# Values in the projections' bank, and two more of the short slots' adds on GpSimd

## The chip, the cores and the metric

The kernel runs on one core of a Trainium2 chip. The metric is the device time of one execution in microseconds. The engines are the tensor engine (PE, matmuls), the vector engine (DVE), the scalar engine (ACT), GpSimd (POOL) and SyncE (SP), which here only issues DMAs. Each works through its own queue in order, and they wait for each other on semaphores. PE writes its results into PSUM, in this kernel eight banks of 128 x 512 fp32.

## The reference, cut to what matters

Eight images of 512 channels and 32 x 32 positions. Layer 0 is attention with 8 heads of 64 channels, layer 1 a masked 3 x 3 convolution. The change touches layer 0 alone.

```python
def _L0_conv_ref(x, Wq, bq, Wk, bk, Wv, bv):
    t = x.reshape(B, C, S).transpose(0, 2, 1)
    q = t @ Wq.T + bq
    k = t @ Wk.T + bk
    v = t @ Wv.T + bv
    q = q.reshape(B * NUM_HEADS, S, hd)          # k and v likewise
    scores = jnp.einsum('gqd,gkd->gqk', q, k) / jnp.sqrt(hd)
    attn = jax.nn.softmax(scores, axis=-1)
    wv = jnp.einsum('gqk,gkd->gqd', attn, v)
    ...
x = x + _L0_conv_ref(_gn(x), Wq, bq, Wk, bk, Wv, bv)
x = x + _L1_conv_ref(_gn(x), weight, bias, mask_weight, filter, 1)
```

The plain reshape into B * 8 groups of 1024 rows makes a group out of 128 tokens by 8 segments of 64 channels. Such a group is one slot of the kernel.

## The kernel before, in words

**Slots and units.** Layer 0 is 64 slots, 8 per image (s = 0 to 7), each 128 tokens. A slot has 8 units, one for each segment of the keys. In a unit PE makes two score tiles of 128 x 512 (`scores`, four matmul steps of two each, L735), ACT takes their exponentials into `prob` (L936), and PE weighs the values with them (`weigh`, L761), two units at a time. In slots 0, 1, 4 and 5 PE also projects keys and queries for the next half image (`project_qk`, 12 matmuls in each of units 1, 3, 5 and 7, L684). In slots 2 and 6 it projects the values (`project_value`, the same count, L694). Slots 3 and 7 have no projection: they are the short slots. Fourteen of them count as short in the code below, those of images 0 to 6.

**Maxima.** During slot h PE also makes, for slot h + 1, eight pairs of tiles (`max_pair`, L705) that DVE reduces to row maxima (`max_item`, L1297). The table `MAX_AT` says in which unit, and whether ahead of its scores (place "a") or behind them (place "c"). In a value slot the pairs stand in units 0, 1, 2, 3, 4, 4, 5, 6, in a short slot in units 0, 1, 2, 2, 3, 4, 4, 5. After the last pair DVE makes a minimum (L1301) and a transposition (L1305), ACT gathers the shift row, and a DMA writes it to where the next slot's scores read it.

**Banks.** Banks 0 to 2 hold scores, banks 3 to 5 are a ring, bank 6 takes the weighed values, and bank 7 (`qk_bank`) the key and query projections; in the short slots it is a fourth score bank as well. The ring is shared by maxima, values, denominators (`den_item`, L1318) and statistics. PE's `take` waits on `ring_free` until DVE has given back the item three before. `PER_RING` is the number of items per image, 146, and since that isn't a multiple of three the distance is two for some items at the end of a period. A pair takes two banks at once, before its first matmul. The rotation of the score banks (`score_banks`) begins each short slot with bank 7. In `scores` PE waits for the banks of both tiles of a unit before it issues either.

**Value copy.** DVE copies a projected value tile out of the ring and adds its bias (`value_item`, L1309). It then waits for its own `value_out` before it frees the bank.

**Sums.** The exponentials are summed in two accumulators. The odd tiles' adds (chunks kc = 1 to 7) are POOL's (L1119). The even tiles' adds are DVE's (L1290), except chunks `EVEN_BY_POOL` in short slots, which are POOL's (`add_even`, L1125). DVE's add of chunk kc stands in unit kc + 1 behind that unit's maxima, and that of chunk 7 in unit 0 of the next slot. In a value slot the add of chunk 6 stands in unit 7, ahead of the fourth value copy. ACT waits for the sums before it overwrites a tile of `prob`, and PE before it makes the denominators. The last five slots of the kernel are summed on PE and have no such adds.

**The start.** Ahead of slot 0 PE projects keys, queries and values of the first half image, the values in four groups of 12 matmuls without a pause, then makes the maxima for slot 0, with the first key projections of the second half in between.

Of the kernel before, what the change touches and what calls it, by code (L numbers as in the profile page):

```python
# [25 lines left out]
ALU = mybir.AluOpType  # L26
# [14 lines left out]
HPI = S // TOK  # L41
# [11 lines left out]
EVEN_BY_POOL = (2, 5)  # L53
# [109 lines left out]
def build(nc, x, wqT, wkT, wvT, chan, bv, wcu, const, out):  # L163
# [11 lines left out]
    with top:  # L175
# [3 lines left out]
        def sb(stack, name, shape, dt):  # L179
# [37 lines left out]
            "u_out0", "u_out1", "u_out2", "den_full", "pv_out", "den_out", "den_in", "recip_done", "recip_out", "recip_in", "o_done", "resid_done", "x1_stored", "value_out")}  # L217
# [107 lines left out]
        PER_RING = HPI * (16 + 1) + 2 * HPH + 2  # L325
# [317 lines left out]
        def _(pe):  # L643
# [21 lines left out]
            def project_qk(t, half, which, j, first=False):  # L665
# [5 lines left out]
                if first:  # L671
                    dst = (qk_bank, pv_bank)[j % 2]
                    if which + j > 0:
                        pe.wait_ge(s1["qk_out"], 4 * which + j)
                else:
                    pe.wait_ge(s1["qk_out"], 8 * t + 4 * which + j + 1)
                    if which == 0 and j == 0:
                        pe.wait_ge(s1["exp_done"], 4 + 16 * HPH * (t - 1))
                steps = [(a, b, c) for c in range(NC) for a, b in
# [8 lines left out]
            def project_value(t, half, g):  # L688
                pe.wait_ge(s1["xn_split"], 2 + 4 * (t + 1))
                dst = take()  # L690
# [5 lines left out]
                mm.then_inc(s1["ring_full"], 1)  # L696
# [22 lines left out]
            def scores(h, s, u, part):  # L719

                half, tok = tokens(s)
                for e in range(2):
                    n = 16 * h + 2 * u + e
                    if part == 0:
                        pe.wait_ge(s1["exp_done"], 4 + n + 1 - score_ago[n])
                        if score_turn[n] == 3:
                            pe.wait_ge(s1["qk_out"], 1 + 8 * (h // HPH + 2))
                for n in (2 * part, 2 * part + 1):
# [11 lines left out]
            def sum_prob(h, kc):  # L740

                if kc == 0:
                    pe.wait_ge(s1["qk_out"], 1 + 16 * B)
                    pe.wait_ge(s1["den_out"], h)
# [368 lines left out]
        def _(pool):  # L1113
# [7 lines left out]
            def add_even(h, s, kc):  # L1121
# [3 lines left out]
                nc.gpsimd.tensor_tensor(acc, acc, prob[:, (2 * kc) % 8], ALU.add).then_inc(s1["sum0"], 1)  # L1125
# [128 lines left out]
        def _(dve):  # L1254
# [52 lines left out]
            def value_item(h, half, g):  # L1307
                src = item()
                dve.scalar_tensor_tensor(out=val[half][:, g], in0=src[:], scalar=1.0 / WSCALE, in1=bv_row[:],  # L1309
                                         op0=ALU.mult, op1=ALU.add).then_inc(s1["value_out"], 1)  # L1310
                dve.wait_ge(s1["value_out"], h + 1)
                dve.sem_inc(s1["ring_free"], 1)
# [507 lines left out]
```

## Time and profile before

| | us |
|---|---|
| median of 3 runs | 2551.43 (2547.43 to 2552.20) |
| the profiled execution | 2547.02 |
| its span, first to last instruction | 2545.2 |
| PE busy | 2440.3 (96%) |
| DVE busy | 1947.8 (77%) |
| ACT busy | 1146.8 (45%) |
| POOL busy | 1156.7 (45%) |

Slot 0 of image 0 begins some 73 us into the span, and the convolution follows from about 1792 us on. TensorE's granted clock has a mean of 0.997. A matmul's time in the rows is its latency: back to back ones begin 0.22 apart and last 0.38. Rows of DVE work that follow each other without a wait overlap by some 0.08, so single maxima of 0.68 begin 0.60 apart. "[0.53 <-DVE nmax L1297]" is the idle time of the engine ahead of a row and what ended it.

### The profile page before, as it was taken

The numbers are of one execution on the slowest core, as the hardware profiler recorded it, in microseconds if no ns is written. First come the engines' busy times: TensorE is split into PE (matmuls) and PEld (weight loads), VectorE is DVE, ScalarE is ACT, GpSimd is POOL, SyncE is SP. The second block draws the span as 40 slices with busy tenths as digits, with TensorE's granted clock in tenths as the row PEclk, the third lists the DMA queues.
The fourth block names the chain that finished last, engine by engine and source line by source line (L and its number), as shares of the span: only waits on it lengthen the run. The fifth ranks groups of instructions, "written<-read, shape, count | busy, mean of one in ns | idle before, by whom it ended". The sixth has DMA issues, their size and how long they took to land.

```text
span 2545.2 us, 38904 instructions
## 1 busy us (share of the span) xinstructions
PE 2440.3 (96%) x13768; PEld 916.8 (36%) x13768; DVE 1947.8 (77%) x2617; ACT 1146.8 (45%) x2059; POOL 1156.7 (45%) x998
## 2 busy tenths in 40 slices
PE   6899999999999999999999999988999999999999
PEld 2233333333333333333333333322444444444444
DVE  5887887888888788788878898976856967967415
ACT  4455556555555556555555554565232132132100
POOL 1376577567567657756755764653121030030000
PEclk9999999999999999999999999999999999999999
DMA  4213232131322313213132231322534634633534
GB/s 128 73 53 87 68 99 81 37 106 53 95 76 74 87 47 111 82 45 106 50 98 76 75 110 36 106 71 72 191 135 174 236 132 165 231 133 133 205 110 165
DMA packets 162783, 267.95 MB, mean 105 GB/s; under 512 B 80160, under 2 KB 80288, under 8 KB 162592
## 3 DMA queue, kind: packets, MB, share of 16 engines
q1 hardware_dynamic: 162320, 264.41, 31.5%
q8 instruction: 113, 1.85, 0.3%
q10 hardware_dynamic: 272, 1.05, 0.1%
q14 instruction: 78, 0.64, 0.1%
HBM read 195.54 MB, written 52.69 MB: 98 GB/s over the span
## 4 chain that ended last, share of the span: by engine, by line
PE 76%; DVE 16%; issue 4%; ACT 1%; DMA 1%; POOL 1%; SPq 0%; DVEq 0%; ACTq 0%; POOLq 0%
PE bank L854 29%; PE bank L761 13%; PE bank L684 12%; PE bank L735 12%; DVE nmax L1297 6%; PE bank L694 5%; DVE prob_sum L1290 4%; PE bank L705 4%; DVE val L1309 1%; PE bank L715 1%; DVE xn_lo L1274 1%; DMA q_top<-shift 1%; ACT prob L936 1%; PE bank L748 1%; DVE xn L1367 1%
## 5 line engine op out<-in xcount | busy, mean ns | idle before, releaser
L1297 DVE TENSOR_REDUCE nmax<-bank 128x1 f32<-128x512 f32 x1024 | 650.9, 680 | 201.6 <-PE bank L705 188.5
L936 ACT ACTIVATE prob<-bank 128x512 f32<-128x512 f32 x1024 | 555.2, 594 | 467.1 <-PE bank L735 465.5
L854 PE MATMUL bank<-v,u_slab 128*128 128x512 f16 x3456 | 746.9, 379 | 0.0
L1119 POOL TENSOR_TENSOR prob_sum<-prob_sum,prob 128x512 f32<-128x512 f32 x354 | 489.8, 1384 | 256.7 <-ACT prob L936 254.6
L761 PE MATMUL bank<-prob,val 128*64 128x512 f32 x2048 | 495.9, 605 | 0.0
L854 PEld LDWEIGHTS bank<-v,u_slab 128*128 128x128 f16 x3456 | 338.1, 98 | 406.9 <-issue 0.8
L1290 DVE TENSOR_TENSOR prob_sum<-prob_sum,prob 128x512 f32<-128x512 f32 x326 | 364.2, 1117 | 23.1 <-POOL prob_sum L1125 21.5
L705 PE MATMUL bank<-k_hi,q_hi 64*128 64x512 f16 x1024 | 200.2, 385 | 35.5 <-DVE nmax L1297 34.7
L735 PE MATMUL bank<-q_hi,k_hi 64*128 64x512 f16 x1024 | 196.4, 378 | 26.4 <-ACT prob L936 26.3
L761 PEld LDWEIGHTS bank<-prob,val 128*64 128x64 f32 x2048 | 124.2, 136 | 237.8 <-issue 186.5
L735 PE MATMUL bank<-q_lo,k_hi 64*128 64x512 f16 x1024 | 196.2, 378 | 8.6 <-DMA q_top<-shift 8.5
L684 PE MATMUL bank<-xn_hi,w_hi 128*128 128x512 f16 x512 | 196.2, 383 | 7.8 <-DVE xn_lo L1274 7.8
L735 PE MATMUL bank<-q_top,spare 64*128 64x512 f16 x1024 | 196.0, 377 | 0.0
L735 PE MATMUL bank<-q_hi,k_lo 64*128 64x512 f16 x1024 | 195.8, 377 | 0.0
L684 PE MATMUL bank<-xn_lo,w_hi 128*128 128x512 f16 x512 | 195.0, 381 | 0.0
L684 PE MATMUL bank<-xn_hi,w_lo 128*128 128x512 f16 x512 | 194.8, 381 | 0.0
L924 ACT ACTIVATE qk<-bank,prm 128x512 f32<-128x512 f32 x128 | 87.9, 687 | 207.7 <-PE bank L684 207.7
L266 POOL TENSOR_TENSOR rstd<-ve,fixed 128x4 f32<-128x4 f32 (+1 forms) x12 | 17.4, 1450 | 337.5 <-DVE ve L247 337.5
L705 PEld LDWEIGHTS bank<-k_hi,q_hi 64*128 64x128 f16 x1024 | 53.1, 93 | 321.5 <-DVE nmax L1297 161.8
L1131 POOL TENSOR_TENSOR den_sb<-pv_sb,den_sb 128x512 f32<-128x512 f32 x64 | 95.2, 1488 | 155.7 <-DMA den_sb<-recip_scratch 155.1
L1119 POOL TENSOR_TENSOR prob_sum<-prob 128x512 f32<-128x512 f32 x59 | 74.7, 1265 | 180.9 <-ACT prob L936 177.9
L1002 ACT ACTIVATE y<-bank 128x512 f32<-128x512 f32 x48 | 28.3, 597 | 276.0 <-PE bank L854 250.4
(146 smaller groups left out, 2876.5 us busy)
## 6 DMA issues: line engine op xcount, KB each, us to landing
u_slab<-u_scratch SPq DMA_DIRECT2D x72, 1024.0 KB, 4.7
xs<-x SPq DMA_DIRECT2D x28, 1024.0 KB, 5.5
tile<-x_scratch SPq DMA_DIRECT2D x26, 1024.0 KB, 6.5
u_scratch<-u_w SPq DMA_DIRECT2D x96, 192.0 KB, 2.9
den_sb<-recip_scratch SPq DMA_DIRECT2D x128, 128.0 KB, 2.9
x_scratch<-xr SPq DMA_DIRECT2D x16, 1024.0 KB, 4.3
xr<-x SPq DMA_DIRECT2D x15, 1024.0 KB, 7.8
res<-x_scratch SPq DMA_DIRECT2D x14, 1024.0 KB, 7.3
```

What stands on the lines that cost most here:

```text
L684: mm = pe.matmul(dst[:], a[:, w, c, j * P:(j + 1) * P], b[:, half, c], start=(n == 0), stop=(n == len(steps) - 1))
L694: mm = pe.matmul(dst[:], a[:, half, c, g * TOK:(g + 1) * TOK], b[:, 2, c], start=(n == 0), stop=(n == len(steps) - 1))
L705: pe.matmul(dst[e][:].rearrange("p (k t) -> p k t", t=TOK), q_hi[half][rows, n // 2, tok], k_hi[half][rows, NC * part:NC * part + NC, tok] ...
L735: mm = pe.matmul(dst[:].rearrange("p (j t) -> p j t", t=TOK), k_op, q_op, start=(n == 0), stop=(n == 3))
L761: pe.matmul(pv_bank[e * D:(e + 1) * D, :], val[s // HPH][:, s % HPH, kc * D:(kc + 1) * D], prob[:, (2 * kc + e) % 8], start=(kc == 0), sto ...
L854: mm = pe.matmul(bank_at(pos, co)[:].rearrange("p (i n) -> p i n", i=2), slab[:, l, c, co * P:(co + 1) * P], image[v][:, 2 * c:2 * c + 2, ...
L924: act.activation(qk32[:, j % 2], src[:], ACT.Identity, bias=prm[:, col:col + 1], scale=1.0 / WSCALE).then_inc(s1["qk_full"], 1)
L936: act.activation(prob[:, (2 * u + e) % 8], score_bank[score_turn[16 * h + 2 * u + e]][:], ACT.Exp, scale=float(D) ** -0.5).then_inc(s1["ex ...
L1119: nc.gpsimd.tensor_tensor(acc, in0, prob[:, (2 * kc + 1) % 8], ALU.add).then_inc(s1["sum1"], 1)
L1131: nc.gpsimd.tensor_tensor(den_sb[:], pv_sb[:], den_sb[:], ALU.mult).then_inc(s1["o_done"], 1)
L1290: dve.tensor_tensor(acc, in0, prob[:, (2 * kc) % 8], ALU.add).then_inc(s1["sum0"], 1)
L1297: dve.tensor_reduce(nmax[:, seg, part:part + 1], src[:], AX.X, ALU.max, negate=True)\
```

## The change

Three edits. First, the value projections write into bank 7 in place of a ring bank. PE waits there for the last query projection to be copied out (`qk_out`) and for the value tile before (`value_out`); DVE waits on a semaphore of its own (`value_ready`) and no longer frees a ring bank. Second, whoever uses bank 7 next waits for the last value copy: the next half's first projection, the short slot's scores in bank 7, and the sums on PE of the last slots. The ring has 138 items per image. Third, POOL takes the even adds of chunks 1, 2, 4 and 5 in short slots; the add of chunk 1 reads `prob` twice, as the first of a sum.

```diff
-EVEN_BY_POOL = (2, 5)
+EVEN_BY_POOL = (1, 2, 4, 5)
...
-        PER_RING = HPI * (16 + 1) + 2 * HPH + 2
+        PER_RING = HPI * (16 + 1) + 2
...
                     if which == 0 and j == 0:
                         pe.wait_ge(s1["exp_done"], 4 + 16 * HPH * (t - 1))
+                        pe.wait_ge(s1["value_out"], 4 * t)
...
             def project_value(t, half, g):
                 pe.wait_ge(s1["xn_split"], 2 + 4 * (t + 1))
-                dst = take()
+                pe.wait_ge(s1["qk_out"], 1 + 8 * (t + 1))
+                pe.wait_ge(s1["value_out"], 4 * t + g)
+                dst = qk_bank
...
-                mm.then_inc(s1["ring_full"], 1)
+                mm.then_inc(s1["value_ready"], 1)
...
                         if score_turn[n] == 3:
                             pe.wait_ge(s1["qk_out"], 1 + 8 * (h // HPH + 2))
+                            pe.wait_ge(s1["value_out"], 4 * (h // HPH + 2))
...
                     pe.wait_ge(s1["qk_out"], 1 + 16 * B)
+                    pe.wait_ge(s1["value_out"], B * HPI)
...
-                nc.gpsimd.tensor_tensor(acc, acc, prob[:, (2 * kc) % 8], ALU.add).then_inc(s1["sum0"], 1)
+                in0 = prob[:, 0] if kc == 1 else acc
+                nc.gpsimd.tensor_tensor(acc, in0, prob[:, (2 * kc) % 8], ALU.add).then_inc(s1["sum0"], 1)
...
             def value_item(h, half, g):
-                src = item()
-                dve.scalar_tensor_tensor(out=val[half][:, g], in0=src[:], scalar=1.0 / WSCALE, in1=bv_row[:],
+                dve.wait_ge(s1["value_ready"], h + 1)
+                dve.scalar_tensor_tensor(out=val[half][:, g], in0=qk_bank[:], scalar=1.0 / WSCALE, in1=bv_row[:],
                                          op0=ALU.mult, op1=ALU.add).then_inc(s1["value_out"], 1)
-                dve.wait_ge(s1["value_out"], h + 1)
-                dve.sem_inc(s1["ring_free"], 1)
```

PE at the turn from a value slot to a short slot, before: the end of the fourth value projection, unit 0's max pair, and the first scores.

```order
500 L694 MATMUL bank<-w_lo,xn_hi 128x512
501 L694 MATMUL bank<-w_hi,xn_lo 128x512
502 L705 MATMUL bank<-k_hi,q_hi 128x512 [waits ring_free,qk_split,qk_moved]
503 L705 MATMUL bank<-k_hi,q_hi 128x512
504 L735 MATMUL bank<-q_hi,k_hi 128x512 [waits exp_done,qk_out]
505 L735 MATMUL bank<-q_hi,k_hi 128x512
506 L735 MATMUL bank<-q_hi,k_lo 128x512 x2
```

And of the change, the same place:

```order
500 L697 MATMUL bank<-w_lo,xn_hi 128x512
501 L697 MATMUL bank<-w_hi,xn_lo 128x512
502 L708 MATMUL bank<-k_hi,q_hi 128x512 [waits ring_free,qk_split,qk_moved]
503 L708 MATMUL bank<-k_hi,q_hi 128x512
504 L739 MATMUL bank<-q_hi,k_hi 128x512 [waits value_out,exp_done,qk_out]
505 L739 MATMUL bank<-q_hi,k_hi 128x512
506 L739 MATMUL bank<-q_hi,k_lo 128x512 x2
```

The order is the same. The first score matmul of the short slot has a third semaphore to wait for, `value_out`.

PE ahead of slot 0, where the second of the four value projections begins, before and then of the change:

```order
109 L694 MATMUL bank<-w_lo,xn_hi 128x512
110 L694 MATMUL bank<-w_hi,xn_lo 128x512
111 L694 MATMUL bank<-w_hi,xn_hi 128x512 [waits ring_free,xn_split]
112 L694 MATMUL bank<-w_lo,xn_hi 128x512
113 L694 MATMUL bank<-w_hi,xn_lo 128x512
```

```order
109 L697 MATMUL bank<-w_lo,xn_hi 128x512
110 L697 MATMUL bank<-w_hi,xn_lo 128x512
111 L697 MATMUL bank<-w_hi,xn_hi 128x512 [waits value_out,qk_out,xn_split]
112 L697 MATMUL bank<-w_lo,xn_hi 128x512
113 L697 MATMUL bank<-w_hi,xn_lo 128x512
```

In place of the ring's `ring_free` it waits for the copy of the tile before, `value_out`.

POOL in a short slot, before, up to the odd add of chunk 7, which stands in the next slot (L1119 odd tiles, L1125 even tiles, L1131 the division for the slot before, L1138 its residual):

```order
63 L1119 TENSOR_TENSOR prob_sum<-prob 128x512 [waits sum1,exp_done]
64 L1125 TENSOR_TENSOR prob_sum<-prob_sum,prob 128x512 [waits sum0,exp_done]
65 L1119 TENSOR_TENSOR prob_sum<-prob_sum,prob 128x512 [waits sum1,exp_done] x3
66 L1125 TENSOR_TENSOR prob_sum<-prob_sum,prob 128x512 [waits sum0,exp_done]
67 L1119 TENSOR_TENSOR prob_sum<-prob_sum,prob 128x512 [waits sum1,exp_done]
68 L1131 TENSOR_TENSOR den_sb<-pv_sb,den_sb 128x512 [waits recip_in,pv_out]
69 L1119 TENSOR_TENSOR prob_sum<-prob_sum,prob 128x512 [waits sum1,exp_done]
70 L1138 TENSOR_TENSOR xr<-xr,den_sb 128x4x128 [waits o_done]
71 L1119 TENSOR_TENSOR prob_sum<-prob_sum,prob 128x512 [waits sum1,exp_done]
```

And of the change (L1124 odd, L1131 even, L1137 and L1144 the division and the residual):

```order
63 L1131 TENSOR_TENSOR prob_sum<-prob 128x512 [waits sum0,exp_done]
64 L1124 TENSOR_TENSOR prob_sum<-prob 128x512 [waits sum1,exp_done]
65 L1131 TENSOR_TENSOR prob_sum<-prob_sum,prob 128x512 [waits sum0,exp_done]
66 L1124 TENSOR_TENSOR prob_sum<-prob_sum,prob 128x512 [waits sum1,exp_done] x2
67 L1131 TENSOR_TENSOR prob_sum<-prob_sum,prob 128x512 [waits sum0,exp_done]
68 L1124 TENSOR_TENSOR prob_sum<-prob_sum,prob 128x512 [waits sum1,exp_done]
69 L1131 TENSOR_TENSOR prob_sum<-prob_sum,prob 128x512 [waits sum0,exp_done]
70 L1124 TENSOR_TENSOR prob_sum<-prob_sum,prob 128x512 [waits sum1,exp_done]
71 L1137 TENSOR_TENSOR den_sb<-pv_sb,den_sb 128x512 [waits recip_in,pv_out]
72 L1124 TENSOR_TENSOR prob_sum<-prob_sum,prob 128x512 [waits sum1,exp_done]
73 L1144 TENSOR_TENSOR xr<-xr,den_sb 128x4x128 [waits o_done]
74 L1124 TENSOR_TENSOR prob_sum<-prob_sum,prob 128x512 [waits sum1,exp_done]
```

Two even adds join, those of chunks 1 and 4, each ahead of the odd add of its chunk.

## Rows read from the trace of the kernel before

**Rows 1.** The page's first part: busy time, share of the span and instructions.

```profile
PE 2440.3 (96%) x13768; PEld 916.8 (36%) x13768; DVE 1947.8 (77%) x2617; ACT 1146.8 (45%) x2059; POOL 1156.7 (45%) x998
```

**Rows 2.** Stretches, image 3's slots 2, 3, 5, 6, 7: length, engines' busy time, clock.

```profile
769.86:799.31 29.45, 28.72 (x172) 9.68 (x169) 25.76 (x35) 19.46 (x37) 23.88 (x24) 1.00 0.16 42
799.31:818.81 19.50, 18.03 (x124) 5.86 (x121) 16.89 (x27) 9.67 (x21) 11.50 (x10) 1.00 0.31 94
...
847.35:875.84 28.49, 28.48 (x172) 9.74 (x169) 21.06 (x31) 17.34 (x36) 20.27 (x19) 1.00 0.52 152
875.84:905.34 29.50, 28.59 (x171) 9.77 (x168) 24.89 (x34) 16.83 (x31) 15.29 (x12) 1.00 0.11 27
905.34:925.16 19.82, 18.02 (x123) 5.94 (x119) 17.22 (x28) 9.66 (x21) 9.13 (x8) 1.00 0.19 68
```

**Rows 3.** Timeline of PE, image 4, slots 2 and 3: start, length, instruction, idle before.

```profile
994.85 0.38 PE L694 MATMUL bank<-w_hi,xn_hi 128*128 128x512 f16 x1 [0.17 <-DVEq L1320]
...
999.31 0.39 PE L705 MATMUL bank<-k_hi,q_hi 64*128 64x512 f16 x2 [0.53 <-DVE nmax L1297]
...
1011.79 0.38 PE L694 MATMUL bank<-w_hi,xn_lo 128*128 128x512 f16 x1
...
1012.33 0.38 PE L735 MATMUL bank<-q_hi,k_hi 64*128 64x512 f16 x2
...
1017.19 0.39 PE L705 MATMUL bank<-k_hi,q_hi 64*128 64x512 f16 x2 [0.78 <-DVE nmax L1297]
```

**Rows 4.** Timeline of DVE, image 4, slots 2 and 3.

```profile
997.63 0.69 DVE L1309 SCALAR_TENSOR_TENSOR val<-bank,bv_row 128x512 f32<-128x512 f32 x1 [0.79 <-PE bank L694]
998.47 1.29 DVE L1297 TENSOR_REDUCE nmax<-bank 128x1 f32<-128x512 f32 x2
...
1009.70 3.43 DVE L1290 TENSOR_TENSOR prob_sum<-prob_sum,prob 128x512 f32<-128x512 f32 x2
1013.06 0.68 DVE L1309 SCALAR_TENSOR_TENSOR val<-bank,bv_row 128x512 f32<-128x512 f32 x1
...
1021.80 3.79 DVE L1297 TENSOR_REDUCE nmax<-bank 128x1 f32<-128x512 f32 x6 [0.74 <-PE bank L705]
```

**Rows 5.** Timeline of DVE, image 1, end of slot 2: the fourth value copy.

```profile
371.88 0.69 DVE L1309 SCALAR_TENSOR_TENSOR val<-bank,bv_row 128x512 f32<-128x512 f32 x1
```

**Rows 6.** Timeline of PE, image 1, slot 3 and slot 7: the pair of unit 2.

```profile
376.88 0.39 PE L705 MATMUL bank<-k_hi,q_hi 64*128 64x512 f16 x2 [0.79 <-DVE nmax L1297]
...
483.78 0.39 PE L705 MATMUL bank<-k_hi,q_hi 64*128 64x512 f16 x2 [1.14 <-DVE nmax L1297]
```

**Rows 7.** Timeline of DVE, slot 7 of image 1 and of image 4: fourth value copy.

```profile
479.65 0.68 DVE L1309 SCALAR_TENSOR_TENSOR val<-bank,bv_row 128x512 f32<-128x512 f32 x1
...
1118.87 0.68 DVE L1309 SCALAR_TENSOR_TENSOR val<-bank,bv_row 128x512 f32<-128x512 f32 x1
```

**Rows 8.** Timeline of PE, image 4, slots 6 and 7.

```profile
1108.71 0.38 PE L694 MATMUL bank<-w_hi,xn_hi 128*128 128x512 f16 x1 [0.22 <-DVE nmax L1297]
...
1123.00 0.39 PE L705 MATMUL bank<-k_hi,q_hi 64*128 64x512 f16 x2 [0.58 <-DVE nmax L1297]
```

**Rows 9.** Timeline of PE ahead of slot 0: first and last value matmul, next projection.

```profile
45.28 0.38 PE L694 MATMUL bank<-w_hi,xn_hi 128*128 128x512 f16 x1
...
55.42 0.38 PE L694 MATMUL bank<-w_hi,xn_lo 128*128 128x512 f16 x1
...
56.05 0.39 PE L684 MATMUL bank<-xn_hi,w_hi 128*128 128x512 f16 x1
```

**Rows 10.** Timeline of DVE ahead of slot 0: last query's split, fourth value copy.

```profile
46.84 0.69 DVE L1282 TENSOR_TENSOR q_lo<-qk,q_hi 128x512 f16<-128x512 f32 x1 [1.90 <-ACT q_hi L927]
...
55.84 0.69 DVE L1309 SCALAR_TENSOR_TENSOR val<-bank,bv_row 128x512 f32<-128x512 f32 x1 [0.99 <-PE bank L694]
```

**Rows 11.** Timeline of POOL, image 4, slot 3: the even add of chunk 5.

```profile
1029.57 1.26 POOL L1125 TENSOR_TENSOR prob_sum<-prob_sum,prob 128x512 f32<-128x512 f32 x1 [3.06 <-DVE prob_sum L1290]
```

**Rows 12.** Line L1290's instructions: DVE's adds, duration in ns, min/median/max.

```profile
L1290 DVE TENSOR_TENSOR prob_sum<-prob_sum,prob x326: 659/1020/1792, 86.9 to 1666.7; 128x512 f32<-128x512 f32 x163
```

More of the change, by code:

```diff
@@ L216, in build @@
             "u_in", "u_act", "u_pool",
-            "u_out0", "u_out1", "u_out2", "den_full", "pv_out", "den_out", "den_in", "recip_done", "recip_out", "recip_in", "o_done", "resid_done", "x1_stored", "value_out")}
+            "u_out0", "u_out1", "u_out2", "den_full", "pv_out", "den_out", "den_in", "recip_done", "recip_out", "recip_in", "o_done", "resid_done", "x1_stored", "value_ready", "value_out")}
         def statistics(dve, signal, step, cols):
```

## The prediction, made before the changed kernel had run

> **What bounds the kernel now.** I read the page first: the tensor engine (PE) is busy for 2440.3 of 2545.2 us [rows 1]. A gain can only come out of the idle time that is left on it. The table of stretches by slot puts that time in its place [rows 2]. In image 3, slot 5 lasts 28.49 us with PE busy for 28.48, so nothing can be won there. Slots 2 and 6, the ones with value projections, last 29.45 and 29.50 with 0.73 and 0.91 idle. The short slots 3 and 7 last 19.50 and 19.82 with 1.47 and 1.80 idle. Some 5 us of idle time per image, 40 in all, is what the change can reach at most; part of it is the turn from a short to a long slot, which the change leaves as it is.
>
> The timeline of PE names the waits [rows 3, 6, 8]. In image 4's slot 2 a value projection waits 0.17 for a ring bank that the copy of the denominators holds, and the max pair of unit 4 waits 0.53 for the vector engine (DVE). In slot 3 the first max pair of unit 2 waits 0.78 (0.79 in image 1), in slot 7 of image 4 0.58 and in slot 7 of image 1 1.14, all for a DVE max. In slot 6 one more value projection waits 0.22, where the ring's period ends and its banks come round after two items. So PE is held by DVE's lateness around the turn from the value slot to the short slot. The timeline of DVE shows why it is late: the value copy of unit 7 comes behind two adds of 1.7 us each [rows 4, 7], where the same add takes 0.66 at best [rows 12].
>
> **Part 1, values in the projections' bank, in the value slots.** PE issues the same matmuls in the same order. Gone is the ring's wait before each value projection, and gone is DVE's wait for its own copy before it gives a ring bank back: from the copy at 997.63 to the next max at 998.47 are 0.84 [rows 4], where back to back ones are 0.60 apart, so 0.24 per copy.
> - First wait of slot 2: the start comes 0.17 sooner by the idle time shown, 0.24 by the distance of starts. I take 0.24.
> - The max pair of unit 4 still needs the bank of unit 4's first pair, the ring being three deep, and DVE reads that one after the value copy. It was released 0.84 after DVE began on it (998.47 to 999.31, rows 3 and 4). With the projection 0.24 earlier and 0.24 of sync gone it begins at 997.99, so the pair starts at 998.83, or 0.48 sooner than now. This stall is halved, not removed.
> - Slot 6 has the same two and the 0.22 (0.29 by starts): 0.77.
>
> So PE reaches the end of slot 2 about 0.48, and of slot 6 about 0.77, sooner.
>
> **Part 1, at the start of the short slots.** Here the change adds a wait. The four-bank rotation of a short slot begins with bank 7, and both score tiles of unit 0 wait before either is issued. They now wait for the value copy out of bank 7. Queued behind that wait on PE are all scores, the sums of the slot before and the next max pairs; the scalar engine (ACT) waits for those scores. The price: PE's last value matmul starts at 1011.79 and the first score at 1012.33 [rows 3]. A value copy starts at 55.84 after its last matmul's start at 55.42 [rows 9, 10], 0.42 later, and DVE gives a bank back 0.84 after it began (above), so the score starts 1.26 after the matmul at the best, against 0.54: at least 0.72 lost in each of 14 short slots. Where DVE is late it is more.
>
> What it covers is the later wait for the max. Call V the start of unit 7's value copy. Now the pair of unit 2 starts at V + 4.13 (1013.06 and 1017.19; 1118.87 and 1123.00; 479.65 and 483.78) [rows 3, 4, 7, 8], in image 1's slot 3 at V + 5.00 (371.88 and 376.88) [rows 5, 6]. After the change, with the copy at V', the first score starts at V' + 0.84, and without a wait the pair is 4.08 behind it (1017.19 less 0.78, less 1012.33), so it starts at V' + 4.92. The change therefore gains only if the copy comes earlier by more than 0.79, or where the old distance was 5.00.
> - Slot 3, five images like image 1 (images 1, 2, 3, 5 and 6), where the copy waits for PE only: V' is 0.48 earlier, gain 5.00 + 0.48 - 4.92 = 0.56, five times 2.8 us.
> - Slot 3 of images 0 and 4, where the copy waits for DVE: the copy is earlier by 0.48 and the sync, 0.72: a loss of 0.07. I take 0.
> - Slot 7, seven times: earlier by 0.77 and the sync, 1.0, which gives 0.2. The upper end is a copy as early as PE allows: then the first score comes 0.72 late, no wait follows, and the gain is 0.6 where the copy was earliest (1118.87) and some 1.5 where it was latest (479.65). The lower end is one more meeting with an add on GpSimd (POOL), 1.1 us (an add of 1.7 for one of 0.66), a loss of 0.9. I take 0.4, near the row for the plain shift, since an earlier DVE meets a POOL that starts by a DMA's landing and not by DVE: 2.8 us.
> - Image 7 has one value slot and no short slot: 0.5.
>
> The loop gains 2.8 + 2.8 + 0.5 = 6.1 us.
>
> **Part 1, at the beginning.** Four value projections now run back to back from three banks, 45.28 to 55.42 [rows 9]. In one bank the first must wait for ACT's copy of the last query, which ends when DVE takes it up at 46.84 [rows 10]: 1.6 us, with the hop 1.7. Each of the next three must wait 1.26 from the last matmul instead of the usual 0.22: 3.1 us. The first projection of the next half tile (56.05) [rows 9] waits for the fourth copy too: 0.6 us. No slack follows, for the maxima, the shift rows and the first scores all hang on it. Sum: 5.4 us lost once, with nothing to hide it.
>
> **Part 2, two more even adds on POOL.** In 14 short slots the adds of chunks 1 and 4 leave DVE and join POOL, 28 adds at 1.27 [rows 11]: 36 us of POOL work. On DVE they took 0.66 to 1.79 each [rows 12]. Is either on the path? After the pair of unit 2, PE waits for no DVE result in a short slot; DVE is idle in its middle. The 0.79 in front of unit 2 lies before the add of chunk 1. So the relief is worth 0. On POOL's side: at 1029.57 it had sat idle for 3.06 us, waiting for DVE's add of chunk 4 [rows 11]. Now it makes that add itself and starts on chunk 5 no later, so ACT's waits on the sums and the denominators' matmul in the next slot see the same times. I take 0. The bounds: a gain of 0.5 per short slot, about 7 us, if I am wrong that DVE is idle there, and a loss of as much if POOL ends later by one add where ACT needs it.
>
> DVE's add takes from 0.66 to 1.79 us [rows 12], and its longest fall where POOL is adding as well. The Trainium skill (SBUF — State Buffer, "Who interferes with whom") has a rule for this that speaks against part 2: a vector instruction with two inputs in SBUF and a GpSimd one that reads SBUF exclude each other for the whole instruction. By that rule moving an add to POOL takes one off DVE and puts a block in front of another. The trace agrees as to size (0.66 against up to 1.79).
>
> **Sum.** 6.1 gained, 5.4 lost, 0 for part 2: 0.7 us less. Against the profiled execution (2547.02 us) that gives 2546.3. The median of the runs is 4.4 above that execution, and I carry the difference over: 2551.43 - 0.7, about 2550.5.
>
> **The rivals.**
> - *No change to speak of* (as above), 2546 to 2555. For it: the bank's new wait is forced by the order of the banks, and the halved stall by the depth of the ring.
> - *DVE comes clear.* The copies of unit 7 start as soon as PE is done in all 14 short slots. Then slot 3 gains 0.56 seven times and slot 7 about 1.0 seven times, 10.9 with nothing lost but 5.4, and part 2 may give a few tenths per short slot: 5.5 to 10 us less, 2541 to 2546. For it: the sum of DVE's work falls. Against it: the adds of 1.7 us stay in the value slots, where part 2 moves nothing.
> - *The bank's wait costs more than it covers* (slower). If POOL's work meets DVE's last adds of slots 2 and 6 as now or worse, V' is less than 0.79 earlier than V. From that point every tenth is lost fourteen times. With V' only 0.3 earlier in nine of the slots they lose 0.5 each, 4.5 us, and with the 5.4 and the five slots' gain of 2.8 the kernel is 7 slower: 2558.
> - *Adds on POOL block DVE* (slower). If the 28 adds each hold one two-input instruction of DVE for the 1.1 us between 0.66 and 1.79, that is 31 us of DVE. With a quarter on the path it costs 7 to 8: 2558. Against it: maxima read PSUM and keep their 0.60 beside POOL.
> - *The change does less than it says*: the ring stalls stay and only the beginning is paid, 5.4 slower, 2557. I count it with the slower ones.
>
> **How the numbers follow.** No change to speak of 0.54, DVE comes clear 0.25, the bank's wait 0.12, blocking 0.05, less than it says 0.04. A measurement of this kernel tells 0.2% (5.1 us) from no change. Faster by more 0.25, within it 0.54, slower by more 0.21. The range of 8 in 10 goes from 2541.5 (nearly all of the fast case) to 2558 (the slow ones' centre).
>
> **What would show it.** In the changed kernel's profile: the first value matmul of the run at about 47.0 and the next ones 3.6 us apart; the first shift row some 5 us later. In slot 2 no wait before a value projection, and one of about 0.4 before unit 4's second pair. At the start of slots 3 and 7 a wait for the value copy of 0.7 to 1.5, and none before unit 2's pair. Short slots about as long as now, value slots 0.5 to 0.8 shorter. POOL busier by 36 us and its wait of 3 us gone. I am wrong if short slots still show both waits (slower), or if they end up shorter than 19.3 us (faster).

## The result, and the profile after

The changed kernel takes 2555.43 us (median of 20 runs, 2550.62 to 2561.80), the kernel before 2550.61 on the same chips (20 runs, 2545.52 to 2555.19). The ratio is 1.002, with a 95% interval from 1.0013 to 1.0027: about 5 us slower. The prediction said 2550.5 from a base of 2551.43, that is 0.7 less, with 54% on no change. The time fell inside the range (up to 2558.0), but on the slower side, to which it gave 21%.

The profiled execution of the changed kernel took 2560.39 us, near the top of its runs. Its terms below are therefore read slot by slot and not as one sum. The page's first part, beside [rows 1]:

```profile
PE 2451.5 (96%) x13768; PEld 914.6 (36%) x13768; DVE 1916.4 (75%) x2589; ACT 1148.8 (45%) x2059; POOL 1184.4 (46%) x1026
```

DVE lost 28 instructions and 31.4 us, POOL gained 28 and 27.7 us. PE has the same 13,768 matmuls and is "busy" for 11.2 us more, and that alone says that something slowed matmuls. The table of stretches, image 3's slots 2 to 7 (beside [rows 2]) and then slots 7 of image 4 and 0 of image 5; columns as there:

```profile
777.21:807.03 29.82, 29.11 (x171) 9.76 (x170) 23.48 (x36) 19.66 (x37) 23.81 (x28) 1.00 0.17 46
807.03:825.76 18.73, 18.03 (x120) 5.71 (x120) 16.05 (x25) 9.44 (x20) 14.16 (x12) 1.00 0.30 97
825.76:854.61 28.85, 28.37 (x166) 9.57 (x166) 20.22 (x31) 16.80 (x35) 21.95 (x20) 1.00 0.10 24
854.61:883.11 28.50, 28.49 (x169) 9.75 (x168) 21.05 (x31) 17.34 (x35) 20.11 (x19) 1.00 0.53 152
883.11:913.02 29.91, 28.94 (x171) 9.83 (x170) 24.74 (x36) 17.10 (x31) 16.00 (x12) 1.00 0.10 27
913.02:931.75 18.73, 18.03 (x120) 5.71 (x120) 14.94 (x25) 9.44 (x20) 11.73 (x10) 1.00 0.22 72
1127.55:1147.89 20.34, 19.67 (x120) 5.98 (x120) 14.92 (x25) 9.44 (x20) 11.41 (x10) 0.92 0.17 63
1147.89:1176.75 28.86, 28.38 (x166) 9.59 (x166) 23.42 (x35) 14.27 (x29) 15.90 (x12) 1.00 0.15 47
```

A slot runs from the start of its first score matmul to that of the next slot's. The cuts of this table all lie 0.29 us ahead of those matmuls (1127.55 for the row at 1127.84 below), which leaves the lengths as they are. The new wait stands in front of a short slot's first score, so it lies in the slot before: slots 2 and 6 got longer (29.82 and 29.91 for 29.45 and 29.50), the short ones shorter (18.73 twice for 19.50 and 19.82). Slot 4 is at 28.85, where the kernel before has this line:

```profile
818.81:847.35 28.54, 28.53 (x170) 9.68 (x172) 21.20 (x31) 16.63 (x35) 22.84 (x21) 1.00 0.09 25
```

Slot 7 of image 4 lasts 20.34 at a mean clock of 0.92. Three things, then: the trade between slots 2 and 3 or 6 and 7, which is the forecast one; 0.3 us more in slots 0 and 4, which I had priced at nothing; and a clock that I had not thought of.

The medians over images 1 to 5 of every slot, in the main kernels of the study (us; "start" is the first score matmul of slot 0 of image 0; "loop" is all of layer 0 from there on):

| kernel | start | loop | s0 | s1 | s2 | s3 | s4 | s5 | s6 | s7 |
|---|---|---|---|---|---|---|---|---|---|---|
| before | 73.08 | 1718.54 | 28.54 | 29.31 | 29.45 | 19.50 | 28.54 | 28.49 | 29.50 | 19.82 |
| after | 78.58 | 1726.39 | 28.86 | 29.31 | 30.26 | 18.72 | 28.86 | 28.49 | 29.92 | 18.73 |
| p1_only | 78.56 | 1713.35 | 28.71 | 29.31 | 30.28 | 18.72 | 28.56 | 28.49 | 29.92 | 18.72 |
| p2_only | 72.58 | 1724.87 | 28.88 | 29.31 | 29.58 | 19.50 | 28.87 | 28.49 | 29.50 | 19.83 |
| even_125 | 72.59 | 1724.89 | 28.54 | 29.31 | 30.25 | 19.49 | 28.54 | 28.49 | 29.50 | 19.84 |
| p1_vf7 | 78.39 | 1708.03 | 28.62 | 29.31 | 30.16 | 18.72 | 28.57 | 28.49 | 29.60 | 18.73 |
| rot_p1_start2 | 73.69 | 1713.53 | 29.45 | 29.31 | 29.82 | 18.54 | 29.27 | 28.49 | 28.77 | 19.03 |

**The start.** PE ahead of slot 0, beside [rows 9]: the first matmul of each value projection, then the next key projection.

```profile
47.07 0.38 PE L697 MATMUL bank<-w_hi,xn_hi 128*128 128x512 f16 x1 [1.56 <-ACT q_hi L932]
...
50.70 0.38 PE L697 MATMUL bank<-w_hi,xn_hi 128*128 128x512 f16 x1 [0.88 <-DVE val L1315]
...
61.58 0.38 PE L685 MATMUL bank<-xn_hi,w_hi 128*128 128x512 f16 x1 [0.55 <-DVE val L1315]
```

The second, third and fourth projections each show the same 0.88 and begin 3.63 apart. In all 1.56 + 3 x 0.88 + 0.55 = 4.8 us of idle time, and the first key projection stands at 61.58 where it stood at 56.05 [rows 9]: 5.5 us by the starts. The first 1.56 is not the bank's. At the start the query projections alternate between banks 7 and 6, and the last one lies in bank 6. The changed kernel's count waits for its copy all the same, where bank 7 only needs the copy of the one before.

**The bank's wait.** PE at the turns into slots 3 and 7 of image 4, beside [rows 3, 8]. The first row is the second pair of unit 4.

```profile
1006.84 0.39 PE L708 MATMUL bank<-k_hi,q_hi 64*128 64x512 f16 x2 [0.29 <-DVE nmax L1303]
...
1020.68 0.39 PE L739 MATMUL bank<-q_hi,k_hi 64*128 64x512 f16 x2 [0.66 <-DVE val L1315]
...
1125.31 0.39 PE L708 MATMUL bank<-k_hi,q_hi 64*128 64x512 f16 x2
1127.84 0.39 PE L739 MATMUL bank<-q_hi,k_hi 64*128 64x512 f16 x2 [2.14 <-DVE val L1315]
...
1128.81 3.34 PE L766 MATMUL bank<-prob,val 128*64 128x512 f32 x8
```

Unit 4's wait fell from 0.53 to 0.29, and the waits for a ring bank before a value projection and for unit 2's pair of a short slot are gone. In their place each of the 14 short slots waits for the fourth value copy: nine times 0.66, once 0.98 (slot 7 of image 3), and 2.0 to 2.1 in slot 7 of images 0, 2, 4 and 6. DVE in front of the long one, beside [rows 7]:

```profile
1120.61 1.27 DVE L1307 TENSOR_TENSOR nmin<-nmax 128x8 f32<-128x8 f32 x1
1121.98 0.21 DVE L1311 STREAM_TRANSPOSE shift_blk<-nmin 128x32 f32<-128x32 f32 x1
1122.12 1.51 DVE L1280 TENSOR_TENSOR xn_lo<-xn,xn_hi 128x512 f16<-128x512 f32 x1
1123.55 3.44 DVE L1296 TENSOR_TENSOR prob_sum<-prob_sum,prob 128x512 f32<-128x512 f32 x2
1126.91 0.68 DVE L1315 SCALAR_TENSOR_TENSOR val<-bank,bv_row 128x512 f32<-128x512 f32 x1
```

After its last matmul (start 1124.99) the copy could go at 1125.41, as the others do 0.42 behind theirs. It goes 1.5 us later, because it stands behind the slow adds. From the copy's start to the first score are 0.93 or 0.94 us in all 14 slots.

**The clock.** The last PE row above is the first weighing after the 2.14 us wait: 3.34 us for the eight matmuls that take 1.94 elsewhere. The granted clock falls there to the lower of its two levels, 1.2 GHz, for 3.4 us, and the slot lasts 1.6 us longer than a slot 7 without it (20.34 for 18.72).

### The profile page after: what moved, and what is told of

Read it like the earlier page. It is cut to its first block, busy times and chain, and to the rows that moved or that the text cites. A ratio compares the mean times of both kernels' runs of the same rounds, so it can differ in the third digit from the quotient of the medians.

```text
span 2558.6 us, 38916 instructions
## 1 busy us (share of the span) xinstructions
PE 2451.5 (96%) x13768; PEld 914.6 (36%) x13768; DVE 1916.4 (75%) x2589; ACT 1148.8 (45%) x2059; POOL 1184.4 (46%) x1026
## 4 chain that ended last, share of the span: by engine, by line
PE 79%; DVE 11%; issue 3%; DMA 2%; ACT 2%; POOL 1%; SPq 1%; DVEq 0%; ACTq 0%; POOLq 0%
PE bank L859 29%; PE bank L766 15%; PE bank L739 12%; PE bank L685 11%; PE bank L697 6%; DVE nmax L1303 5%; PE bank L708 5%; DMA q_top<-shift 2%; DVE prob_sum L1296 2%; PE bank L718 1%; DVE nmin L1307 1%; DVE val L1315 1%; ACT shift L950 1%; SPq L425 1%; ACT prob L941 1%
## 5 line engine op out<-in xcount | busy, mean ns | idle before, releaser
L1124 POOL TENSOR_TENSOR prob_sum<-prob_sum,prob 128x512 f32<-128x512 f32 x354 | 487.1, 1376 | 273.0 <-ACT prob L941 273.0
L766 PE MATMUL bank<-prob,val 128*64 128x512 f32 x2048 | 501.5, 611 | 0.0
L1296 DVE TENSOR_TENSOR prob_sum<-prob_sum,prob 128x512 f32<-128x512 f32 x312 | 331.0, 1061 | 15.4 <-POOL prob_sum L1131 13.9
L1137 POOL TENSOR_TENSOR den_sb<-pv_sb,den_sb 128x512 f32<-128x512 f32 x64 | 95.2, 1488 | 159.0 <-DMA den_sb<-recip_scratch 158.5
L999 ACT ACTIVATE v<-v 128x2176 f16<-128x2176 f32 x24 | 48.4, 2015 | 209.2 <-DVE v L1489 102.8
```

Of the source, the lines that this page charges most:

```text
L766: pe.matmul(pv_bank[e * D:(e + 1) * D, :], val[s // HPH][:, s % HPH, kc * D:(kc + 1) * D], prob[:, (2 * kc + e) % 8], start=(kc == 0), sto ...
L1124: nc.gpsimd.tensor_tensor(acc, in0, prob[:, (2 * kc + 1) % 8], ALU.add).then_inc(s1["sum1"], 1)
L1137: nc.gpsimd.tensor_tensor(den_sb[:], pv_sb[:], den_sb[:], ALU.mult).then_inc(s1["o_done"], 1)
L1296: dve.tensor_tensor(acc, in0, prob[:, (2 * kc) % 8], ALU.add).then_inc(s1["sum0"], 1)
```

## The experiments

Every ratio is to the kernel before, timed on the same chip; times are medians.

### Each part alone

`p1_only` is the changed kernel with the old sums:

```diff
-EVEN_BY_POOL = (1, 2, 4, 5)
+EVEN_BY_POOL = (2, 5)
```

> The changed kernel with POOL's even adds left at chunks 2 and 5, so the values' bank alone. Theory A (the loss is the start, some 5 us, and the shift row that POOL's added adds make late, 0.33 us in each of 14 slots after a short slot; the bank's wait itself about pays for what it covers): slot 0 of image 0 begins at about 78.3 as in the changed kernel, slots 0 and 4 last 28.55 us again and not 28.87, the minimum L1307 in slots 3 and 7 takes 0.17 and not 1.02, and the time is some 4 to 5 us below the changed kernel's, at most 1 us above the kernel before. Theory B (the wait for bank 7 at the start of the short slots is the loss): as slow as the changed kernel, 5 us above before.

`p2_only` is the kernel before with the third edit alone, the new `EVEN_BY_POOL` and the first add that reads `prob` twice.

> The kernel before with POOL's even adds of chunks 1, 2, 4 and 5, so the second part alone. Theory A: slots 0 and 4 grow from 28.55 to about 28.87 us by a wait for the shift row, since the minimum in the short slots meets POOL's add and takes 1.0 and not 0.17; everything else as before; 4 to 5 us slower. Theory B, and the forecast on record: POOL's two adds cost nothing, no difference beyond 1 us.

Part 1 alone: 2552.88 us, 1.0005 (0.9995 to 1.0015). Part 2 alone: 2552.91 us, 1.0008 (1.0000 to 1.0016), about 2 us. Neither is far from no change in a timing; the traces say more. In `p1_only` the loop is 5.2 us shorter than before and the start 5.5 later, both close to the forecast terms (6.1 and 5.4). Slots 3 and 7 are at 18.72 to 18.75 in all seven images, slots 2 and 6 carry the new wait. In `p2_only` no slot's median moves by more than 0.13 but those of slots 0 and 4, which go from 28.54 to 28.88, seven times each, as in the changed kernel. So the 0.3 us in slots 0 and 4 come from part 2, and they recur 14 times: 4.6 us in the profile. Why the timings show only some 2 us of it isn't shown.

The reason is at the end of the short slot. DVE of the changed kernel, image 4, slot 3:

```profile
1034.10 1.29 DVE L1303 TENSOR_REDUCE nmax<-bank 128x1 f32<-128x512 f32 x2 [0.21 <-PE bank L708]
1035.43 1.02 DVE L1307 TENSOR_TENSOR nmin<-nmax 128x8 f32<-128x8 f32 x1
1036.55 0.21 DVE L1311 STREAM_TRANSPOSE shift_blk<-nmin 128x32 f32<-128x32 f32 x1
```

POOL at the same time (L1131 are even adds, L1124 odd ones):

```profile
1033.93 1.26 POOL L1131 TENSOR_TENSOR prob_sum<-prob_sum,prob 128x512 f32<-128x512 f32 x1 [1.24 <-DVE prob_sum L1296]
1035.15 1.27 POOL L1124 TENSOR_TENSOR prob_sum<-prob_sum,prob 128x512 f32<-128x512 f32 x1
1036.39 1.26 POOL L1131 TENSOR_TENSOR prob_sum<-prob_sum,prob 128x512 f32<-128x512 f32 x1
```

And who waits for the shift row, PE in the next slot's first unit:

```profile
1040.19 0.39 PE L739 MATMUL bank<-q_lo,k_hi 64*128 64x512 f16 x2 [0.18 <-DMA q_top<-shift]
```

The minimum, two inputs of 128 x 8, takes 1.02 us instead of 0.17. So it is in all 14 short slots (1.01 to 1.03) of every kernel that gives chunk 4's add to POOL, and in all 14 it is 0.17 in every kernel that doesn't. It ends at 1036.45, when POOL's add of chunk 4's odd tile (1035.15 + 1.27) is over. Before, the minimum of the same slot fell into POOL's idle time:

```profile
1028.36 0.17 DVE L1301 TENSOR_TENSOR nmin<-nmax 128x8 f32<-128x8 f32 x1
```

It lies inside the 3.06 us for which POOL sat idle until 1029.57 [rows 11]. Now POOL has chunk 4's even add, pushes the odd add behind it, and fills just that time. The minimum is what the next slot's shift row hangs on: it comes out 0.85 late, of which 0.3 reaches PE. The rest was slack of the shift row before. The Trainium skill (SBUF — State Buffer, "Who interferes with whom") states that a vector instruction with two inputs in SBUF and a GpSimd one that reads SBUF exclude each other for the whole instruction, and that the one issued second waits. The rows agree: the minimum begins at 1035.43, behind the add of 1035.15, and ends with it. They show it for a vector instruction of 0.17 us, and it is the small one that pays; the add takes its usual 1.27.

### Is it chunk 4's add?

`even_125` is `p2_only` with `EVEN_BY_POOL = (1, 2, 5)`: chunk 4 stays with DVE.

> The kernel before with POOL's even adds at chunks 1, 2 and 5: of the two added ones only that of chunk 1, in unit 2. Theory A (it is the add of chunk 4, in unit 5, which meets the minimum of unit 5): slots 0 and 4 last 28.55 us as before and the minimum in the short slots takes 0.17. If the add of chunk 1 shifts POOL's row of adds into it (rival), they last 28.87.

The line L1302 in the list of instruction groups of `even_125` (count, busy time and mean ns of one), with chunk 4's add on DVE:

```profile
L1302 DVE TENSOR_TENSOR nmin<-nmax 128x8 f32<-128x8 f32 x64 | 17.3, 270 | 2.2
```

and of `p2_only`, with it on POOL:

```profile
L1302 DVE TENSOR_TENSOR nmin<-nmax 128x8 f32<-128x8 f32 x64 | 30.1, 471 | 2.2
```

Slots 0 and 4 are back at 28.54. That chunk 4's add makes the minimum late is shown. But the same trace has slot 2 at 30.25 for 29.45, and its one time is 2553.13, so it did not show that chunk 1's add is free. The same kernel was timed:

> The kernel before with the adds of chunks 1, 2 and 5 on POOL, timed. The one look at it showed slots 0 and 4 at the 28.54 us of before (chunk 4's add left DVE's minimum alone) but slot 2 0.8 us longer in that one profile, so it is open whether chunk 1's add is free. If it is free, and chunk 4's carries the whole price of part 2, the time is that of before, 2550.7, ratio 1.000. Rival: chunk 1's add costs too, through what POOL does at the turn and in slot 2, and the time is 2552.5 to 2556 with slot 2 again longer than 30.

2553.48 us, 1.0011 (1.0002 to 1.0020). The rival held: slow by 2.4 us without chunk 4's add, with slot 2 at 30.60. The extra time of slot 2 is a wait of its first unit for the DMA of the shift row: 0.6 to 2.0 us of idle time in images 0 to 6 of both profiles of this kernel, in place of 0.6 and 0.7 in images 1 and 2 and under 0.1 in images 3 to 6 before. The instructions ahead of that DMA stand at the same distance from the slot's start as in the kernel before, and it is issued at the same distance (in image 3, 3.36 us ahead in the one and 3.35 in the other), so it lands later; a 1 MB load of the next image (`xs<-x`) is under way at the time, also as before. Why it lands later with chunk 1's add moved I can't say, and `p2_only`, which moves that add as well, has slot 2 at 29.58. Nor does the wait need that add: `p1_only`, which leaves it with DVE, has 0.5 to 1.2 us of it in images 1, 2, 4 and 6. This stays open. No run gives POOL chunk 4's add without chunk 1's, so how the timed price of part 2 splits between the two isn't shown. What part 2 costs in all was timed three times: 2.0 us on the kernel before (2550.9 to 2552.9), 2.5 on part 1 (2552.9 to 2555.4; 3.8 by the ratios) and 6.4 with the rotation below (2539.5 to 2545.8). In the two profiles of the last case slots 0 and 4 differ by 3.2 us in all; the rest isn't explained.

### The start in two banks

`start2` is the changed kernel with the first four value projections alternating between bank 7 and bank 6, which is free until the first weighing. The waits are set to match, and the first projection then no longer waits for the copy of the last query. PE's side of the edit, where `first` marks those four:

```diff
-                pe.wait_ge(s1["qk_out"], 1 + 8 * (t + 1))
-                pe.wait_ge(s1["value_out"], 4 * t + g)
-                dst = qk_bank
+                pe.wait_ge(s1["qk_out"], 8 * (t + 1) if first and g == 0 else 1 + 8 * (t + 1))
+                if not first or g > 1:
+                    pe.wait_ge(s1["value_out"], 4 * t + g - (1 if first else 0))
+                dst = (qk_bank, pv_bank)[g % 2] if first else qk_bank
```

> The changed kernel, but the four value projections ahead of slot 0 alternate between banks 7 and 6. Theory A: of the 5.2 us lost at the start some 4 come back, slot 0 of image 0 begins at 74 to 75 and not at 78.3, and the rest of the kernel runs as in the changed kernel: 4 us below it. If the start had slack behind it (rival), the slot begins earlier but the median stays at the changed kernel's.

Slot 0 begins at 72.96 instead of 78.58, so the 5 us of the start are gone with the second bank and the looser count. By the idle times above, 3.2 of them are the single bank's and 1.6 the count's; no run tells the two apart. The kernel takes 2552.65 us, 1.0005 (0.9996 to 1.0014), 2.8 less than the change; in the ratios it is 3.8, and the intervals hold 5.

### Another bank first

The short slot's rotation begins with bank 7, in unit 0. `rot2` leaves it out of the choice for unit 0:

```diff
-        b = min(range(4 if short else 3), key=lambda k: seen[k])
+        b = min(range(4 if short and n % 16 >= 2 else 3), key=lambda k: seen[k])
```

> The changed kernel, but in the short slots bank 7 enters the rotation of the score banks only at the third tile (unit 1), so unit 0's scores need no value copy. Theory A: the waits of 0.6 and of 2.1 us ahead of slots 3 and 7 go, and a wait for DVE's max comes back at unit 2 of the short slot; a pair of slots 2 and 3 together changes by less than 0.5 us, but the stretches at half clock that follow the 2.1 us waits (3.4 us long, 1.7 us lost each) go: 3 to 5 us below the changed kernel. Theory B: the waits were the loss; pairs 2 and 3, 6 and 7 each get 0.6 to 2 us shorter, 10 us below the changed kernel or more.

2545.83 us, 0.9981 (0.9970 to 0.9991): 9.6 less than the change. No first score of a short slot waits for the value copy any more, and slot 6 is at 28.77. The gain is smaller than slots 2, 3, 6 and 7 alone would give (22 us in the two profiles), because slots 0 and 4 grow to 29.6 (9 us). PE of `rot2`, image 3, slot 4:

```profile
820.00 0.38 PE L739 MATMUL bank<-q_hi,k_lo 64*128 64x512 f16 x2
821.30 0.39 PE L739 MATMUL bank<-q_lo,k_hi 64*128 64x512 f16 x2 [0.92 <-DMA q_top<-shift]
```

With the new rotation the next slot's scores wait for no exponential at that turn (0.56 us before), and PE runs into the shift row. `rot_p1` takes the sums of before with it, and `rot_p1_start2` the start in two banks too.

> As rot2 (bank 7 enters the short slots' rotation at the third tile), and POOL's even adds at chunks 2 and 5 as before. Theory A (POOL's added adds make the shift row late): the slots after a short one last some 28.7 us and not 29.6, ten microseconds less in all than rot2, and the time is about 2536. If the wait for the shift row in rot2 comes from the rotation and not from POOL's adds (rival), those slots stay at 29.6 and the time at 2545.

> As rot_p1, and the four value projections ahead of slot 0 alternate between banks 7 and 6. Slot 0 of image 0 begins at about 74 and not at 78, 4 us below rot_p1: about 2532, and below the kernel before by 0.7%.

`rot_p1`: 2539.48 us, 0.9955 (0.9942 to 0.9968). `rot_p1_start2`: 2534.84 us, 0.9941 (0.9927 to 0.9955), 16 us faster than the kernel before and 21 faster than the change. Both expectations were some 3 us too low. Slots 0 and 4 stayed at 29.4 instead of falling below 29: PE runs into the shift row at that turn with two adds on POOL as well as with four. It waits there for 0.6 to 1.3 us in `rot_p1` and for 0.9 to 1.0 in `rot2`.

### The copy ahead of the add

`value_first` is `p1_only` with DVE's value copy ahead of the same unit's add, in all four value units.

> The values' bank alone (POOL at chunks 2 and 5, rotation as in the changed kernel), and on DVE the value copy of a unit stands ahead of that unit's add. Theory A (the 2 us waits ahead of some short slots are the copy behind two adds of 1.7 us, and the stretches at half clock follow such waits): slots 2 and 6 all last about 29.6 us, none 30.9, the wait at the start of a short slot is 0.6 everywhere, the mean clock of the runs rises from 0.9963 to about 0.9975, and the time falls by 3 to 6 us against the values' bank alone. If the clock has another cause (rival), it stays at 0.996 while the slots get shorter.

2566.51 us, 1.0061 (1.0049 to 1.0073): it failed. Its list of waits, with total, times and longest:

```profile
PE bank L708 <- DVE nmax L1303: 33.5, 42, 2.2
...
PE bank L739 <- DVE val L1315: 10.9, 14, 1.1
```

The same lines of `p1_only`:

```profile
PE bank L708 <- DVE nmax L1303: 15.7, 27, 2.5
PE bank L739 <- DVE val L1315: 14.0, 14, 2.1
```

The wait that it was made for did fall. But in units 1, 3 and 5 DVE now idles until PE has finished the projection (its waits for that sum to 91.4 us, in `p1_only` to 70.2), its add comes later, and the maxima behind it later still: their wait doubles. So the order was put right only where no maxima follow, in unit 7:

```diff
+                        if place == "d" and u == 7:
+                            for kind, a in items[place]:
+                                if kind == "value":
+                                    value_item(4 * (t + 1) + a, 1 - s // HPH, a)
+                            items[place] = [x for x in items[place] if x[0] != "value"]
```

> Part 1 alone, with DVE's copy of the fourth value tile (unit 7 of a value slot) ahead of that unit's add of chunk 6; the first three copies stay behind their adds. Copies first in all four units had shortened the short slot's first wait (10.9 us in all against 14.0) and lost 18 us elsewhere, which I put down to units 1, 3 and 5, where maxima stand behind the delayed add. If that is right, here the waits for the fourth copy sum to some 10 to 11 us instead of 14, slots 2 and 6 stay below 30.3 and 29.9 (by 0.1 to 0.4), and the time is 1 to 4 us under part 1 alone (2552.9), some 2550. Rival: the add of chunk 6, now later, pushes the maxima of the next slot's unit 0 or ACT's overwriting of prob; then the short slots grow beyond 18.72 by what slots 2 and 6 give, and the time is 2553 or more. A second point on the clock: if the stretches at 1.2 GHz follow the waits of some 2 us, there are none behind a slot's first score here.

2543.82 us, 0.9977 (0.9967 to 0.9986): 9 us less than part 1 alone (7 by the ratios), where I expected 3. DVE of `p1_vf7` at the end of image 4's slot 6, where the change has the 2.14 us wait:

```profile
1115.71 1.76 DVE L1296 TENSOR_TENSOR prob_sum<-prob_sum,prob 128x512 f32<-128x512 f32 x1
1117.56 0.69 DVE L1315 SCALAR_TENSOR_TENSOR val<-bank,bv_row 128x512 f32<-128x512 f32 x1
1118.17 0.98 DVE L1296 TENSOR_TENSOR prob_sum<-prob_sum,prob 128x512 f32<-128x512 f32 x1
```

PE there, and its line in the list of waits:

```profile
1118.50 0.39 PE L739 MATMUL bank<-q_hi,k_hi 64*128 64x512 f16 x2 [0.66 <-DVE val L1315]
```

```profile
PE bank L739 <- DVE val L1315: 9.2, 14, 0.7
```

Every one of the 14 waits is now at its floor. That is 4.8 us less waiting; some 3 more are clock (below). With this one order of two instructions part 1 is worth 7 us net, where without it the kernel took 2 us more, not clear of the noise.

> Part 1 alone, with the two banks for the first four value projections at the start and the rotation as in the change: it stands between part 1 alone and rot_p1_start2, and tells apart what the start and what the rotation are worth. By the start's 4.6 us it comes at 2548 (0.999 of the kernel before), with slot 0 at 73.7. Against rot_p1_start2 it then leaves some 13 us to the rotation. Rival (the start's gain does not add up, since what starts sooner waits later): 2551 to 2553.

2547.70 us, 0.9992 (0.9983 to 1.0001), as expected: the start is worth 5.2 us here and 4.6 between `rot_p1` and `rot_p1_start2`, and the rotation 12.9 and 13.4, each with the other edit and without. They add up.

> rot_p1_start2 with the fourth value copy ahead of the add of chunk 6 in unit 7. There the rotation has already taken the wait for that copy away from the slot's first scores, and bank 7 is wanted first in unit 1. If nothing waits for the fourth copy any more, this changes the time by less than 1.5 us either way: 2535. Rival (the copy is still waited for, in the unit where bank 7 comes in): 1 to 3 us less, 2532 to 2534. Second rival (the later add delays the first maxima): 2 to 5 more.

2537.79 us, 0.9951 (0.9938 to 0.9963), against 0.9941 (0.9927 to 0.9955) without the moved copy. The intervals overlap and the profiled spans stand the other way (2535.8 and 2540.8 us), so no difference is shown. The two remedies do the same work and don't add up.

### The clock

| kernel | clock, mean of its runs | waits of some 2 us (1.97 to 2.14) ahead of a short slot |
|---|---|---|
| after, start2, p1_only, p1_start2 | 0.9960, 0.9961, 0.9963, 0.9960 | 3 or 4 each |
| value_first, p1_vf7, rot2, rot_p1, rot_p1_start2, best_vf7 | 0.9970, 0.9974, 0.9971, 0.9977, 0.9972, 0.9968 | none |
| before, p2_only, even_125_timed | 0.9971 to 0.9975, 0.9974, 0.9970 | none |

I took 13 profiles together (all but that of `even_125_timed`) and looked between 90 and 1760 us, where the loop runs. They have 20 stretches at 1.2 GHz, each of 3.4 us. All 20 begin between 0.1 us before and 1.5 us after the end of a PE wait with 1.96 to 2.56 us of idle time. Such waits are not always followed by one: of the 86 waits of 1.5 us or more, 43 are of 1.95 or more, and the 20 are all among these. This is a count, and which of them are followed changes from run to run: `p1_only` had three such waits ahead of short slots in its profile and no stretch. Seven of the 20 follow the wait ahead of a short slot. Of the other 13, 12 lie in images 6 and 7, where the kernel before has two such waits too. The mean clock of the changed kernel's runs is 0.0010 to 0.0014 under that of the kernel before, which is 2.7 to 3.6 us of 2552 if PE is taken as busy throughout (an estimate).

## Why the prediction was right or wrong, point by point

- **The start**, forecast 5.4 us lost: slot 0 begins 5.5 later, the value projections 3.63 apart (forecast 3.6), the first at 47.07 (47.0). Right in its times. The reason given for the first 1.7, "in one bank the first must wait for ACT's copy of the last query", is not: that tile lies in bank 6, and it is the kernel's count that waits for it.
- **The value slots**, PE at the end of slot 2 and slot 6 earlier by 0.48 and 0.77. From the shift row's matmul in unit 0 to the last value matmul of the slot it is 28.28 us before and 27.81 after in slot 2, 28.53 and 27.80 in slot 6: 0.47 and 0.73. The ring's waits are gone, and unit 4's wait is 0.29 for 0.53 ("one of about 0.4"). Right.
- **The bank's wait**, at least 0.72 in each short slot from a best case of 1.26 between matmul and score. It is 0.42 + 0.94 = 1.36 instead: the hop to the first score was taken from a ring bank's release and is 0.1 longer. That the cover is real was right too: no wait is left at unit 2's pair, and the rival of two waits fell. Short slots were to stay "about as long as now" and value slots to get 0.5 to 0.8 shorter. That sentence was wrong by my own mechanism, since the first score is where a slot ends and the next one begins; the sums of the pairs are what counts. Slots 6 and 7 of seven images together are 4.2 us shorter in `p1_only` than before (2.8 forecast), 2.4 of it in image 6. Slots 2 and 3 together are 1.3 shorter (2.8 forecast), because slot 2's first unit waits for its shift row, in image 4 by 0.5 us and in image 6 by 1.0, where before it had next to no wait.
- **The loop's gain** of part 1, forecast 6.1: 5.2 in the profile of `p1_only`. Right in mechanism and nearly in size. What it hid is its spread: slot 7 was given 0.4 for all seven. In images 1, 3 and 5 the pair of slots 6 and 7 gains 0.7 to 1.5, and in images 0, 2 and 4 it loses 0.2 to 0.9, for there the copy stands behind two slow adds and the first score waits some 2 us. Waits of this length are also the ones that the falls of the clock followed.
- **Part 2**, forecast 0. **This step failed.** I wrote that POOL "makes that add itself and starts on chunk 5 no later, so ACT's waits on the sums and the denominators' matmul in the next slot see the same times". That is true (chunk 5's add begins 15.7 us into the slot for 17.2 before), and it answers the wrong question. I looked at who waits for POOL and not at what DVE does in the time that POOL had been idle. The 3.06 us of idle time [rows 11] were the cover of DVE's minimum. The rule for it stood in the text, was weighed on the adds alone, and its rival had 5%. Its price was put on big adds (31 us of DVE by 28 x 1.1, a quarter on the path); what was hit is one small instruction per short slot, by 0.85 us, with 0.3 on the path. By the timings part 2 is worth 2 to 2.5 us of the 5 (3.8 by the ratios). POOL's busy time rose by 27.7 us, where 36 was forecast.
- **The clock**, not in the forecast at all, some 3 us. The lower clock is measured; that the waits of 2 us bring it rests on the count and on the kernels without such waits, whose mean clock is higher.

The balance of the change against the kernel before: start +5.5, part 2 +2.3 by the timings (+4.6 by the profile's slots), clock about +3, the loop of part 1 -5.2. That is +5.6 with the timed value of part 2, and 4.8 was timed; the agreement is closer than the timed terms are known, whose intervals reach some 0.1%, 2.6 us, to each side. The forecast had the first and the last of them nearly right, which cancel, and the two between at nothing.

## What to carry to other kernels

Idle time on POOL is not free for work if DVE makes a short two-input instruction in it on whose result a long chain hangs: look at what DVE does there, down to the smallest instruction, before something is put in. Where several producers are moved into one bank, the price is set by who stands ahead of the copy out of it in its queue, so move the copy or the next user of the bank first (9 and 13 us here) and the bank afterwards. And a reordering that is right in the unit where no maxima follow (9 us gained) can be wrong in the three where they do (23 us lost between `p1_vf7` and `value_first`). Last, a semaphore count taken over from another place can wait for more than the bank needs, as the first value projection's does.

## What was new about the hardware

- A DVE instruction of 0.17 us with two SBUF inputs of 128 x 8 lasts 1.01 to 1.03 us in each short slot where POOL is adding and up to 1.29 elsewhere, while the POOL add beside it in the rows above keeps its 1.27.
- All 20 falls of the granted clock in the loops (13 profiles) came within 1.5 us of the end of a PE wait of 1.96 to 2.56 us; three of them, in slot 7 of images 0, 4 and 6 of the changed kernel, cost about 1.6 us each.
- The shift row's DMA landed 0.6 us later (image 3, slot 2) in one kernel than in another at the same distance of issue, with a 1 MB load in flight in both. The reason stayed open.
